# A macaron layer with ternary weights: the first half of the FFN's inner columns in 128-column pairs over all tiles of block 0, and six weight pieces loaded as bf16

## The reference

```python
x = x + 0.5 * ffn(layernorm(x), w_gate_up, w_proj)
x = x + attention(layernorm(x), w_qkv, w_proj_attn, b_proj)
x = x + 0.5 * ffn(layernorm(x), w_gate_up, w_proj)

def ffn(x, w_gate_up, w_proj):             # w_gate_up [4096, 512], w_proj [512, 2048]
    gate, up = split(x @ ternary(w_gate_up).T)
    h = silu(gate) * up
    return rms_norm(h) @ ternary(w_proj).T

def ternary(w):                            # in bf16, groups of 64 along a row
    w = bf16(w)
    scale = max(mean(abs(group)), 1e-8)
    w_hat = clip(round(w / scale), -1, 1) * scale
    return w + (w_hat - w)
```

## Time and profile before

| | us |
|---|---|
| median of 3 runs | 894.78 (893.35 to 896.58) |
| the profiled execution, its own time | 892.16 |
| its span in the trace | 890.4 |
| PE busy | 869.2 (98% of the span) |
| DVE busy | 476.0 (53%) |
| ACT busy | 371.0 (42%) |
| POOL busy | 72.2 (8%) |

### The profile page before, as it was taken

How to read it: one execution, slowest core, us unless ns; L and a number is a source line. 1 busy time by engine, 2 the same in 40 slices (tenths; PEclk the granted TensorE clock), 3 DMA queues, 4 the chain that set the end, 5 groups by cost and what they waited for, 6 DMA issues and landing times.

```text
span 890.4 us, 12348 instructions
## 1 busy us (share of the span) xinstructions
PE 869.2 (98%) x4672; PEld 410.3 (46%) x4672; DVE 476.0 (53%) x960; ACT 371.0 (42%) x732; POOL 72.2 (8%) x107
## 2 busy tenths in 40 slices
PE   4899999999999999999999999999999999999998
PEld 3534444444444444454555545444444444444443
DVE  7999997824345444535474737553343444433232
ACT  6677657545434445212121213253334343433331
POOL 3211001200010000100000000000000010000000
PEclk9999999999999999999999999999999999999999
DMA  9898507995435688432221304044433433342235
GB/s 287 120 142 155 90 13 157 199 208 136 95 62 122 123 169 161 94 53 48 43 55 31 64 14 84 13 84 80 87 82 72 71 71 71 71 72 60 60 67 134
DMA packets 251386, 84.95 MB, mean 95 GB/s; under 512 B 237888, under 2 KB 240448, under 8 KB 251328
## 3 DMA queue, kind: packets, MB, share of 16 engines
q1 hardware_dynamic: 242704, 70.54, 41.5%
q0 software_dynamic: 3872, 4.72, 3.9%
q10 hardware_dynamic: 4752, 8.91, 3.1%
HBM read 25.43 MB, written 4.19 MB: 33 GB/s over the span
## 4 chain that ended last, share of the span: by engine, by line
PE 93%; DVE 4%; DMA 1%; issue 0%; SPq 0%; ACT 0%; DVEq 0%
PE proj_ps L1083 25%; PE gate_ps L1069 22%; PE up_ps L1069 22%; PE gate_ps L1174 7%; PE up_ps L1174 7%; PE proj_ps L1093 5%; PE proj_ps L1069 3%; PE gate_ps L1108 1%; PE up_ps L1108 1%; PE sum_ps L1055 1%; DMA xs<-xn 1%; DMA xs<-in_L_attn_x_dram 1%; PE proj_ps L1189 1%; DVE stats L764 0%; DVE att_w L846 0%; DVE att_w L841 0%
## 5 line engine op out<-in xcount | busy, mean ns | idle before, releaser
L1083 PE MATMUL proj_ps<-down_w,slots 128*128 128x512 bf16 x960 | 211.3, 379 | 0.0
L1069 PE MATMUL gate_ps<-gu_w,xT 128*128 128x512 bf16 (+1 forms) x904 | 203.3, 368 | 2.5 <-DVE gu_w L851 1.4
L1069 PE MATMUL up_ps<-gu_w,xT 128*128 128x512 bf16 (+1 forms) x904 | 203.3, 368 | 0.0
L785 DVE SCALAR_TENSOR_TENSOR slots<-up_ps,silu 128x512 f32<-128x512 f32 x118 | 81.6, 691 | 175.9 <-PE up_ps L1069 157.0
L1083 PEld LDWEIGHTS proj_ps<-down_w,slots 128*128 128x128 f16 x960 | 93.9, 98 | 113.1 <-DVE xs L807 0.2
L549 ACT ACTIVATE silu<-gate_ps 128x512 f32<-128x512 f32 x118 | 69.6, 590 | 167.2 <-PE gate_ps L1069 167.0
L1069 PEld LDWEIGHTS gate_ps<-gu_w,xT 128*128 128x128 f16 x904 | 86.1, 98 | 102.2 <-DVE gu_w L851 1.9
L1069 PEld LDWEIGHTS up_ps<-gu_w,xT 128*128 128x128 f16 x904 | 86.1, 98 | 99.1
L559 ACT ACTIVATE o_buf<-slots 128x512 f32<-128x512 f32 x128 | 80.3, 628 | 103.7 <-DVE slots L785 103.1
L807 DVE SCALAR_TENSOR_TENSOR xs<-proj_ps,xs 128x512 f32<-128x512 f32 x32 | 22.1, 691 | 135.2 <-PE proj_ps L1083 135.2
L798 DVE SCALAR_TENSOR_TENSOR slots<-slots,inv 128x512 f16<-128x512 f32 x124 | 91.0, 743 | 2.8 <-ACT slots L570 2.8
(11 more groups left out here) (99 smaller groups left out, 718.3 us busy)
## 6 DMA issues: line engine op xcount, KB each, us to landing
out_dram<-xs SPq DMA_DIRECT2D x16, 256.0 KB, 2.4
slots<-in_L_ffn_w_gate_up_dram ACTq DMA_DIRECT2D x6, 512.0 KB, 7.5
aw_raw<-in_L_attn_w_qkv_dram ACTq DMA_DIRECT2D x12, 256.0 KB, 2.8
aw_raw<-in_L_attn_w_qkv_dram SPq DMA_DIRECT2D x12, 256.0 KB, 3.0
xs<-in_L_attn_x_dram SPq DMA_DIRECT2D x2, 1024.0 KB, 7.1
slots<-slots SPq DMA_TRANSPOSE x76, 4.5
xs<-in_L_attn_x_dram ACTq DMA_DIRECT2D x1, 1024.0 KB, 11.5
aw_raw<-in_L_ffn_w_gate_up_dram POOLq DMA_DIRECT2D x4, 256.0 KB, 7.7
```

The lines of the kernel that those rows point to most:

```text
L785: nc.vector.scalar_tensor_tensor(out=h_rows(i, q), in0=bank(up_ps, j), scalar=GU_OUT, in1=silu_rows(j), op0=ALU.mult, op1=ALU.mult).then_i ...
L1069: mm = nc.tensor.matmul(bank(ps, j)[:, first:first + width], xT(m)[:, t, r, k, :], gu_w[:, k, c:c + width], start=(k + r == 0), stop=(k == ...
L1083: mm = nc.tensor.matmul(proj_ps[:, use % 2, :], h_turned(i)[:, r, j, :], down_w[:, j, :], start=(r + j == 0), stop=(r == 1 and j == HC - 1))
```

## The change

**Pairs.** The first half of the inner columns (q = 0 and 1) of block 0 is now made in eight *slice pairs*: pair p has the 128 columns of piece p for all four tiles, side by side in one bank (`gate_up_slice`). Pairs of block 1 stay one tile by 512 columns, and so do q = 2 and 3. The order of the early pairs is `EARLY_PAIRS`; it starts with slices 0 to 3, then alternates one full pair of block 1 and one slice (pieces 4 to 7). Three hand-written tuples (`MADE_BY`, `EVICTED_BY`, `SQUARED_BY`) say how far PE, the eviction and the squares have come by each step. The first six pairs use two sets of banks, since the third still holds turned pieces.

**Pieces 0 to 5** are loaded as bf16 by POOL and turned by PE in bf16 into half a bank each. ACT takes the absolute value and the sign.

**Ternary arithmetic.** ACT makes the sign of every piece with `ACT.Sign` (`act_signs` returns True for all). DVE's chain is six instructions instead of seven: clip the scale, scale minus size, compare, size plus difference, multiply (kept), multiply by the sign. The mask, the or, and the last subtraction and addition go; a difference and a sum in another place come.

**Queues.** All four tiles of block 0 are loaded on SP's queue. Block 1 is loaded tile by tile by POOL, between its loads of the first pieces. Transposed pieces use three buffers instead of five. Block 1's transposes come before pieces 6 to 9 on SP's queue instead of before 9 to 11. Layer norm of blocks 0 and 1: the subtraction of the mean moves to ACT for tiles 0 and 1 of block 0 and for all of block 1 (`centred`), and the factor rstd goes into `x_high` and `x_low`.

The diff, cut to its core (index arithmetic, semaphores' declarations and renamed calls are left out):

```diff
+def early_pairs():
+    order = [(None, 0, p) for p in range(4)]
+    for p in range(4, 8):
+        order += [(p, 0, None), (None, 1, p)]
+    order += [(i, 1, None) for i in range(TILES, EARLY)]
+    return order + [(i, q, None) for q in (2, 3) for i in range(EARLY)]
...
+TWO_SETS = 6
+SETS = [j % 2 if j < TWO_SETS else (j - TWO_SETS + 2) % 3 for j in range(4 * EARLY)]
 def bank_free(j):
-    return j if j < 4 * EARLY else j + 1
+    before = [k for k in range(max(j - 4, 0), j) if bank_set(k) == bank_set(j)]
+    return before[-1] + 1 + CREDIT if before else min(j, CREDIT)
...
-def pairs_until(p):
-    return ((2, 4, 6, 7))[p - 4] if 4 <= p < 8 else 0 if p < 4 else 8 + 5 * (p - 7) // 4 if p < PIECES else 4 * EARLY
-NORM_STEP = 4,4,5,5
-TURN_X1 = (9, 9, 10, 11)
+MADE_BY = (1, 2, 3, 4, 6, 8, 10, 12, 13, 14, 15, 16, 17, 18, 19, 20, 21, 22, 23, 24, 25, 26, 27, 28, 32)
+EVICTED_BY = (0, 0, 1, 2, 3, 5, 7, 9, 11, 13, 14, 15, 16, 17, 18, 19, 20, 21, 22, 23, 24, 25, 26, 27)
+SQUARED_BY = (0, 0, 0, 1, 2, 4, 6, 8, 10, 12, 13, 14, 15, 16, 17, 18, 19, 20, 21, 22, 23, 24, 25, 27)
+NORM_STEP = (2, 3, 4, 5)
+TURN_X1 = (6, 7, 8, 9)
+def squares_until(p):
+    ready = sum(j < SQUARED_BY[p] for i, q, j in SQUARES)
+    return min(ready, squares_until(p - 1) + 2) if 0 < p < PIECES - 1 else ready
...
@@ sync @@
-                sp.wait_ge(wq_done, p - 4)
-                sp.dma_start_transpose(w_turn[p % 5]...
+                if p >= PE_TURNED + 3:
+                    sp.wait_ge(size_done, p - 2)
+                    wait_sign(sp, p - 3)
+                sp.dma_start_transpose(w_turn[p % 3]...
-            for t in range(2):
+            for t in range(TILES):
                 sp.dma_start(x_tile(0, t), x_v[0][:, t]).then_inc(x0_here[t], 16)
@@ gpsimd @@
-            for t in range(TILES):
-                rstd(0, t)
-            pool.wait_ge(first_here[4], 16)
-            load_piece(PE_TURNED)
...
+            load_first(0)
+            load_first(1)
+            rstd(0, 0)
+            load_first(2)
+            rstd(0, 1)
+            nc.gpsimd.dma_start(x_tile(1, 0), x_v[1][:, 0]).then_inc(x1_here[0], 16)
+            load_first(3)
+            rstd(0, 2)
+            rstd(0, 3)
+            nc.gpsimd.dma_start(x_tile(1, 1), x_v[1][:, 1]).then_inc(x1_here[1], 16)
+            load_first(4)
+            nc.gpsimd.dma_start(x_tile(1, 2), x_v[1][:, 2]).then_inc(x1_here[2], 16)
+            load_first(5)
+            nc.gpsimd.dma_start(x_tile(1, 3), x_v[1][:, 3]).then_inc(x1_here[3], 16)
+            load_piece(6)
+            load_piece(7)
+            rstd(1, 0)
+            load_piece(8)
...
@@ scalar @@
+            def centred(m, t):
...
+                nc.scalar.activation(lnx[:, t % 2, :], x_tile(m, t), ACT.Identity, scale=-1.0,
+                                     bias=mv[:, 2 * t:2 * t + 1]).then_inc(lnx_done, 1)
-                    last = nc.scalar.activation(w_twice[p % 4][:, 512 * s:512 * s + 512], proj_ps[:, s, :], ACT.Abs,
-                                                scale=2.0)
-                    nc.scalar.activation(w_turn[p % 5][:, 512 * s:512 * s + 512], proj_ps[:, s, :], ACT.Copy)\
+                nc.scalar.activation(w_size[p % 4], turned(p), ACT.Abs).then_inc(size_done, 1)
+                nc.scalar.activation(w_sign[p % 4], turned(p), ACT.Sign).then_inc(sign_done, 1)
+            def size(p):
+                act.wait_ge(wt_here[p % 3], 16 * ((p - PE_TURNED) // 3 + 1))
+                if p >= 4:
+                    act.wait_ge(near_done, p - 3)
+                nc.scalar.activation(w_size[p % 4], w_turn[p % 3], ACT.Abs).then_inc(size_done, 1)
+            def sign(p):
+                if p >= 4:
+                    act.wait_ge(wq_done, p - 3)
+                nc.scalar.activation(w_sign[p % 4], w_turn[p % 3], ACT.Sign).then_inc(sign_done, 1)
...
             for p in range(PIECES):
+                made = step_pairs(EVICTED_BY, p)
+                for j in made[:1]:
+                    silu_gate(j)
                 for t in norms(p):
+                    centred(1, t)
                     x_high(1, t)
+                if p + 3 < PE_TURNED:
+                    first_size(p + 3)
+                    first_sign(p + 3)
+                if PE_TURNED <= p + 3 < PIECES:
+                    size(p + 3)
+                if p:
+                    group_means(p + 2)
+                for j in made[1:]:
+                    silu_gate(j)
+                if PE_TURNED <= p + 3 < PIECES and act_signs(p + 3):
+                    sign(p + 3)
+                for i, q in step_squares(p):
+                    square(i, q)
@@ vector @@
+            def difference(p):
+                    nc.vector.tensor_tensor(w_scale[p % 3], w_scale[p % 3], w_size[p % 4], ALU.subtract)
             def over_half(p):
-                nc.vector.tensor_tensor(w_twice[p % 4], w_twice[p % 4], w_scale[p % 3], ALU.is_gt)
+                nc.vector.tensor_tensor(w_kept[p % 2], w_size[p % 4], w_scale[p % 3], ALU.is_gt)
+            def near(p):
+                nc.vector.tensor_tensor(w_scale[p % 3], w_size[p % 4], w_scale[p % 3], ALU.add)
+            def kept(p):
+                nc.vector.tensor_tensor(w_kept[p % 2], w_kept[p % 2], w_scale[p % 3], ALU.mult)
...
             def final_weights(p):
-                nc.vector.tensor_tensor(place, shape(w_turn[p % 5]), shape(w_hat), ALU.add)
+                wait_sign(dve, p)
+                    last = nc.vector.tensor_tensor(place, shape(w_kept[p % 2]), shape(w_sign[p % 4]), ALU.mult)
...
                 over_half(p)
+                if p == 0:
+                    x_low(0, 3)
+                for j in soon[:1]:
+                    hidden_early(j)
+                near(p)
+                if p < 2:
+                    kept(p)
+                    for t in new:
+                        x_low(1, t)
+                    final_weights(p)
+                    least_scale(p + 1)
+                    difference(p + 1)
+                else:
+                    least_scale(p + 1)
+                    kept(p)
+                    for j in soon[1:]:
+                        hidden_early(j)
+                    difference(p + 1)
+                    for t in new:
+                        x_low(1, t)
+                    final_weights(p)
+                for j in made[len(soon):]:
+                    hidden_early(j)
@@ tensor @@
+            def gate_up_slice(j, p, tiles=range(TILES)):
+                for t in tiles:
+                    if p == 0:
+                        pe.wait_ge(xT_here[t], 16)
+                    for ps, done, used, at in ((gate_ps, gate_done, gate_used, 0), (up_ps, up_done, up_used, HID)):
+                        if t == 0:
+                            pe.wait_ge(used, bank_free(j))
+                        for k in range(DC):
+                            for r in range(2):
+                                mm = nc.tensor.matmul(bank(ps, j)[:, P * t:P * t + P], xT0[:, t, r, k, :],
+                                                      gu_w[:, k, at + P * p:at + P * p + P], ...
...
+            for p in range(PIECES + 1):
+                pairs = step_pairs(MADE_BY, p)
+                if p < 3:
+                    gate_up_early(p, range(0, 1))
+                    group_sums(p + 3)
+                    if p + 4 < PE_TURNED:
+                        turn_first(p + 4)
+                    gate_up_early(p, range(1, TILES))
+                else:
+                    for j in pairs[:1]:
+                        gate_up_early(j)
+                    group_sums(p + 3)
+                    for j in pairs[1:]:
+                        gate_up_early(j)
```

390 lines of the change are left out of this document (201 added, 189 removed).

## The result

| | before | after |
|---|---|---|
| median of 4 runs each, us | 894.50 (893.35 to 896.58) | 900.88 (900.17 to 901.79) |
| profiled execution, its span, us | 892.16, 890.4 | 901.79, 900.0 |
| first projection starts, us | 148.85 | 156.61 |
| from there to the end, us | 741.5 | 743.4 |

The ratio is 1.0078 (95% interval 1.0061 to 1.0095). The forecast was 890.9, its range ended at 898.5, and the sign is wrong. Of the 9.6 us by which the span grew, 7.8 lie ahead of the first projection and 1.9 behind it. The profiled executions lie further apart than the medians: the one of the kernel before (892.16 us) is faster than all four behind its median, the one of the kernel after (901.79) is the slowest of its four.

What follows compares the result with a forecast made beforehand. PE was taken to bound the kernel; its work 124.8, idle 16.9 and stalls 1.5, 1.0 and 0.7 put the projection at 144.9 us against 148.85, so 894.78 less 3.9 gives 890.9 us, range 884.5 to 898.5.

Steps and rivals of the forecast that it cites:

- the fifth sums: When PE starts the sums behind slice 0; 25.3 us by the forecast.
- When PE can start in earnest: Slice 0 needs block 0's four turned tiles; fourth lands at 23.5 us (ends 19 and 29.7), leaving PE 16.9 us idle.
- the second rival: No gain: transposes beside POOL's full queue land as late as before, fourth at 29.7 us; 897 us, chance 0.20.
- its own sign of being wrong: Block 0's fourth turned tile landing before 20 or after 28 us, or PE's steps 8 to 23 above 4.1 us each.
- SP's queue: Transposes of pieces 6 to 9 stand behind block 1's; costs nothing, piece 6's sizes being ready some 3 us early.
- Two squares in four steps: ACT's steps 9 to 12: 0.61 us more each, 2.4 us in all; 0.7 us of PE stall allowed, 0 to 4.
- The rival in which ACT sets the pace of all sixteen steps: Steps 8 to 23: ACT waits for PE's sums, 4.62 us a step instead of 3.89; 902.6 us, chance 0.12.
- Both kernels do the same work: From the first projection on nothing differs, so the span is that projection's start plus 741.5 us.
- The first piece: POOL's bf16 load starts about 1 us later than before; first finished piece at about 17 us, between 15 and 20.
- the bf16 turn: PE's turn of one early piece in bf16: 0.45 us, six of them 2.7 us, with 0 to 5.2 as ends.
- DVE's step: DVE's step with one pair takes 3.94 us against PE's 3.89; costs nothing while its lag stays under two steps.
- PE's work: Pairs, slice pairs, sums and turns ahead of the first projection: 124.8 us, 1.7 less than before.

Runs made afterwards that it cites:

- e6: Changed kernel with POOL's later loads held back, block 1's transposes at their old places, one square a step, fourth x tile on ACT's queue: 888.85 us, ratio 0.9955.
- e1: Changed kernel with POOL's loads of block 1's x tiles and pieces 6 to 9 held back until block 0 is turned: 899.18 us, ratio 1.0055.
- e2: Changed kernel with block 1's transposes back at their old places on SP's queue (before pieces 9, 9, 10, 11): 895.06 us, ratio 1.0016.
- e4: Changed kernel with at most one square a step on ACT from step 8 on, instead of two: 898.76 us, ratio 1.0048.
- e5: Changed kernel with block 0's fourth x tile loaded on ACT's queue at the start instead of SP's: 899.20 us, ratio 1.0064.
- e7: e6 plus ACT making the high half of block 0's fourth tile before the second piece's size, sign and means: 888.74 us, ratio 0.9949.
- b1: Kernel before, with PE waiting for all four turned tiles of block 0 ahead of slice 0's second tile: ratio 1.0098.
- e8: e7 with DVE instead of ACT making the signs from piece 6 on: ratio 0.9999 to the kernel before.
- e9: Changed kernel with only POOL's loads of pieces 6 to 9 held back until block 0 is turned: 900.70 us, ratio 1.0068.
- e3: Changed kernel with 64 small unused matmuls on PE between slice 0's first tile and the rest of slice 0: 898.09 us, ratio 1.0046.

## Why the prediction was wrong

The forecast had the last turned tile at 23.5 us; then PE had that tile of slice 0 and one of the next slice to do (1.8 us), so the fifth sums came at 25.3, and the projection at 144.9. It came at 156.6, 11.7 us later: 6.8 up to the fifth sums (32.1) and 4.9 behind them. Another 1.9 us lie behind the projection. These 13.6 us are the profile's; the medians are 10.0 us apart (900.88 and 890.9). The four edits of e6 together take off 11 us (0.0123), and leave it at 0.9955, where the forecast had 0.996: what the forecast missed is in these four. Two steps failed outright, the landing of the transposes and the order on SP's queue; the second cost the most in time.

- **When PE can start in earnest: this step failed.** The text put the last turned tile at 23.5 us: "The first lands about 5 us later (between 3.1 and 8.0), at 12, the rest one in 3.9". The first took 9.6 us; the fourth was issued at 17.5 us, behind DVE's wait for its high half, took 11.1 and was turned at 28.6. With the loads held back (e1) it was issued at 17.0 and turned at 20.1. Of the 6.8 us, 5.2 are that (28.68 instead of 23.5), and 1.6 are four lots at the lower clock, 0.4 each, which no step had. The mechanism was the one of the second rival: the transposes land late while the loads run beside them, and an earlier issue was spent in a longer landing (e1). 28.6 us is also past the 28 that the prediction named as its own sign of being wrong. At 27 us that rival gave 894.4 and at 29.7 897, so by itself it would have been near no change, and on its own the mend is worth only 2.1 us in time (e1).
- **SP's queue: this step failed, and cost the most.** The text said of the transposes of block 1 that "this costs nothing while PE starts at 23.5", because piece 6's sizes are ready 3 us before PE needs them. PE started later still, and it cost 5.5 us all the same (e2). The margin was reckoned for piece 6 alone; the fourth of block 1's transposes waits for DVE until 55.43 us, and pieces 9 to 11 are behind it.
- **ACT: right in kind, mis-sized.** The step itself was 3.89 us in the forecast, and PE's steps with one square are 3.89. Two squares in four steps were put at 0.7 us of stall; they are 2.0 (e4). The rival in which ACT sets the pace of all sixteen steps did not happen.
- **"Both kernels do the same work" from 148.85 us on: the work, yes, the time, no.** ACT's queue, which the change empties of its early loads, takes 3.32 us for its first issue, and that is 1.9 us at the end (e5). The loads that moved were counted on the queues that they moved to, not on the one that they left.
- **The first piece** landed at 8.72 us, 2.5 us after the 6.23 of before, not 1; the first finished piece was at 19.66 us, not 17, because DVE waited 1.61 us for the high half of tile 3, a wait that the text had named. Neither set the time here: e7 mends the second and gains nothing more.
- **Right:** the bf16 turn at full clock (22.99 to 23.43 us is 0.44, forecast 0.45); DVE's step, 3.94 us; and PE's work. The turns before it and slice 0's first tile took twice as long (from 20.25 us two lots 0.85 us apart), which the text did not have; it fell into time that PE had to wait anyway. From the fifth sums to the projection the forecast has 119.6 us less stalls of 3.2, 116.4. The profile has 124.5 less six waits of 5.7 in all and 1.6 of slow clock at 65.87 us, 117.2; e7, with two waits of 0.68 and 1.27 us, has 116.6. So of the 4.9 us behind the fifth sums 2.5 are waits beyond those forecast, 1.6 clock, and 0.8 weren't traced. One table load as before, of 1.28 us in the whole program: Sign needs no other than Silu. The Trainium skill (ScalarE: Activation LUTs, Table sets) says that cheap functions are in every set, and names relu, copy, identity and abs; the trace agrees for Abs and Identity, and shows the same for Sign and Square, which the page doesn't name there.

With the four causes and the first piece's order mended, e7 starts its projection at 144.46 us, and the forecast said 144.9. The plan's arithmetic of the work held; what it lacked was mostly in the queues. That the two meet to 0.4 us is partly luck: e7's fifth sums start at 25.95 us, 0.6 later than in the forecast, and its stalls behind them are 2.0 us instead of 3.2.

Against the kernel before, the change also makes PE wait for all four tiles where two were enough. With the fourth landing at 29.7 us that need alone costs 7.6 us there (b1). It isn't dear by itself: e7 has the same need, its transposes land 4.6 to 7.3 us after their issue, PE doesn't wait for any of them, and it beats the kernel before by 0.5%.

## What to carry to other kernels

When a change makes the first useful work depend on more transfers, ask what else is in flight just then, and let loads that aren't needed soon wait for the ones that are; issuing the first transpose 3.1 us sooner beside such loads brought its landing only 1.5 us forward here (16.4 instead of 17.9). Before moving a transfer ahead of others on an in-order queue, look at which engine it waits for: everything behind it inherits that wait, and a late piece can make the next transfer late in turn. And a lag that costs nothing step by step (DVE at 4.28 us against 3.89) isn't free if the end of the stage waits for that engine.

## What was not expected of the hardware

- The first issue on ACT's DMA queue was dear when it came late: 3.32 us at 156.7 us, against 0.38 at 0.87 us in e5 and 0.33 there at 155.6 us, with the same program around it. Why, no run shows.
- After a wait of 3.27 us (after), 3.81 us (e8) or 6.85 us (b1), and after two of 1.90 and 1.27 us close together (e5), TensorE ran at its lower clock for several lots; after waits of 0.61 us (e2), 1.70 us (e9), 1.62 and 0.74 us (e4) and 1.45 us with filler ahead (e3) it did not. A wait of 1.80 us went both ways: the 64 matmuls behind it took 5.37 us in after and e5 and 3.75 us in e1, e4 and e9. So a wait that a timeline shows can cost nearly as much again behind it.
- A DMA transpose of one tile landed in 3.1 us in e1, issued at 17.0 us with the loads of block 1 and the later pieces held back, and in up to 15.5 us (17.3 in e3) beside four tile loads and the weight pieces.
